# Attention output loaded chunk by chunk a pass ahead, maxima transposed with 128 stationary columns, and VectorE's side work moved within a group

## What is computed

```
x = x + attention(layernorm(x)) @ Wo      # 32 query heads, 8 key/value heads, head size 16,
                                          # rotary embedding, causal mask, softmax over the keys
x = x + (silu(xn @ W_gate.T) * (xn @ W_up.T)) @ W_down.T    # xn = layernorm(x), 1376 hidden features
```

## Time and profile before

| | us |
|---|---|
| median of 3 runs | 799.4 (798.14 to 801.4) |
| the profiled execution | 799.8 |
| its span | 798.1 |
| TensorE busy in it | 763.0 (96%) |
| VectorE busy | 441.1 (55%) |
| ScalarE busy | 341.8 (43%) |
| GpSimd busy | 211.5 (27%) |

### The profile page before, as it was taken

The page is one execution under the profiler, slowest core; times in us unless marked ns, Lnnn a source line. Parts: engine busy times, 40 slices in busy tenths (PEclk is TensorE's granted clock), DMA queues, the critical chain, the costliest instruction groups (busy, mean ns, idle before and its releaser), DMA issues.

```text
span 798.1 us, 12148 instructions
## 1 busy us (share of the span) xinstructions
PE 763.0 (96%) x4240; PEld 507.8 (64%) x4240; DVE 441.1 (55%) x984; ACT 341.8 (43%) x684; POOL 211.5 (27%) x384
## 2 busy tenths in 40 slices
PE   4699999999999997999799999999999999999998
PEld 3545444554444443454588888888878888788886
DVE  7787878788877786996445543233322243231212
ACT  3427767766876776668533222111121111121111
POOL 3326763577446753234300000000000000000000
PEclk9959999999999999899999999999999999999999
DMA  7437777234423436370286101412005120030001
GB/s 263 110 89 247 211 239 217 68 85 121 117 78 100 121 100 197 113 209 27 92 252 181 56 14 52 132 42 65 27 1 168 43 79 26 0 106 0 1 1 53
DMA packets 74613, 81.84 MB, mean 103 GB/s; under 512 B 8720, under 2 KB 58384, under 8 KB 74352
## 3 DMA queue, kind: packets, MB, share of 16 engines
q1 hardware_dynamic: 73264, 79.98, 32.8%
q10 hardware_dynamic: 1296, 1.18, 0.6%
HBM read 57.02 MB, written 33.36 MB: 113 GB/s over the span
## 4 chain that ended last, share of the span: by engine, by line
PE 50%; DVE 0%; issue 0%; DVEq 0%
PE bank L1495 35%; PE ps_y L1547 15%; PE bank L1534 1%; DVE x_in L1477 0%; DVEq L1476 0%
## 5 line engine op out<-in xcount | busy, mean ns | idle before, releaser
L734 ACT ACTIVATE probs<-ps_t 128x512 f32<-128x512 f32 (+1 forms) x352 | 184.2, 562 | 89.9 <-PE ps_t L1145 89.6
L869 DVE CUSTOM_DVE_ANT_0 ps_s<-ps_s,mask_row 128x512 f32<-128x512 f32 (+1 forms) x240 | 145.4, 643 | 42.4 <-PE ps_s L1113 41.2
L1113 PE MATMUL ps_s<-k_rows,q_rows 96*128 96x256 bf16 (+3 forms) x512 | 146.8, 316 | 5.7 <-DMA q_rows<-scratch_q_parts 3.7
L1452 DVE TENSOR_TENSOR h<-h,bank 128x512 f32<-128x512 f32 (+1 forms) x44 | 30.3, 688 | 218.9 <-PE bank L1495 217.7
L1145 PE MATMUL ps_t<-q_rows,k_rows 98*128 98x512 bf16 (+1 forms) x352 | 129.4, 371 | 7.3 <-DMA q_rows<-m_t 4.5
L1390 ACT ACTIVATE h<-bank 128x512 f32<-128x512 f32 (+1 forms) x44 | 26.3, 599 | 149.3 <-PE bank L1495 149.3
L642 POOL TENSOR_SCALAR_AFFINE_SELECT probs<-probs 128x512 f32<-128x512 f32 x128 | 84.4, 659 | 0.0
L873 DVE TENSOR_REDUCE m_raw<-ps_s 128x2 f32<-128x512 f32 (+3 forms) x112 | 73.2, 677 | 19.7 <-PE ps_s L1118 19.2
L1158 PE MATMUL ps_o<-probs,v_ones 128*32 128x512 f32 (+3 forms) x1024 | 82.6, 441 | 0.2 <-ACT o_sb L744 0.2
L1396 ACT CAST h_hi<-h 128x512 fp32r<-128x512 f32 (+1 forms) x44 | 27.3, 621 | 128.4 <-DVE h L1452 128.4
L223 POOL TENSOR_TENSOR var_eps<-mean_var,eps 128x1 f32<-128x1 f32 x16 | 3.1, 191 | 289.6 <-DVE mean_var L218 289.6
(11 more groups left out here) (154 smaller groups left out, 1380.6 us busy)
## 6 DMA issues: line engine op xcount, KB each, us to landing
scratch_o<-o_sb SPq DMA_DIRECT2D x31, 256.0 KB, 2.3
q_rows<-scratch_q_parts SPq DMA_DIRECT2D x32, 192.0 KB
x_in<-in_x SPq DMA_DIRECT2D x16, 256.0 KB, 4.6
q_rows<-scratch_q_parts SPq DMA_DIRECT2D x32, 128.0 KB
x_res<-in_x SPq DMA_DIRECT2D x16, 256.0 KB, 2.7
o_in<-scratch_o SPq DMA_DIRECT2D x64, 64.0 KB
inverse<-scratch_inverse SPq DMA_DIRECT2D x64, 64.0 KB
out<-x_in SPq DMA_DIRECT2D x16, 256.0 KB, 2.1
```

Source lines behind the costliest of these rows:

```text
L734: nc.scalar.activation(probs[:, g % 2, heads * u:heads * (u + 1), CHUNK_AT[c]:CHUNK_AT[c + 1]], ps_t[:, pos % S_BANKS, 0:heads * CHUNK_N[c ...
L869: nc.vector.tensor_tensor_reduce(out=bank, in0=bank, in1=mask_row[:, T - width:T], scale=1.0, scalar=LOWEST, op0=ALU.add, op1=ALU.max, acc ...
L1113: mm = nc.tensor.matmul(bank[:, place], q_rows[r][0:ROWS, j, P * q:P * (q + 1)], k_rows[r][0:ROWS, 0:width], start=(place == 0), stop=mask ...
L1452: nc.vector.tensor_tensor(h[0:m, r], h[0:m, r], bank[units["up", f] % BANKS][0:m, :], ALU.mult).then_inc(h_ready, 1)
```

## The change

The attention output's tiles 0 and 1 of batch 0 are loaded in pass 2, one chunk in a slot, and `wo` and the residual tiles at its slot 20. Tiles 2 and 3 are loaded in the last pass, chunk by chunk from slot 9 and slot 13. The load of the first weights of phase 2 moves from slot 14 to slot 16. `m_parts` gets zeros in 96 more columns, so that the stationary operand of the transposition has 128 and it writes 128 rows, of which 32 are read. The transposition stands behind the dense piece of its place instead of ahead of it. `max_low` comes after VectorE's second maximum of slot 0 instead of after the first. The statistics, mean and application of the layernorm, one third part of rotated rows and the reciprocals move to other slots.

```diff
-LO_SLOT = {7: 0, 13: 1, 15: 2, 22: 3, 25: 4}
+LO_SLOT = {7: 0, 14: 1, 15: 2, 22: 3, 25: 4}
-X_SLOT, STATS_SLOT, MEAN_SLOT, APPLY_SLOT = 26, 8, 12, 18
-SUMS_SLOT, INVERSE_SLOT = 7, 16
-WO_HI, WO_LO, O_LOAD, CTX_SCALE, CTX_HI, CTX_LO = 2, 4, 0, 5, 6, 7
+X_SLOT, MEAN_SLOT = 26, 14
+STATS_AT, APPLY_AT = {6: 0, 7: 1, 10: 2, 11: 3}, {18: 0, 19: 1, 22: 2, 23: 3}
+SUMS_SLOT, INVERSE_SLOT = 7, 18
+WO_HI, WO_LO, CTX_SCALE, CTX_HI, CTX_LO = 2, 4, 5, 6, 7
+WO_LOAD = 20
+O_LOAD_AHEAD = {2: [(0, 0)], 3: [(0, 1)], 6: [(0, 2)], 7: [(0, 3)], 10: [(1, 0)], 11: [(1, 1)], 18: [(1, 2)],
+                19: [(1, 3)]}
+O_LOAD = {9: [(2, 0)], 10: [(2, 1)], 11: [(2, 2), (2, 3)], 13: [(3, 0)], 14: [(3, 1)], 15: [(3, 2), (3, 3)]}
-FFN_LOAD, FFN_HI, FFN_LO = 14, 19, 25
+FFN_LOAD, FFN_HI, FFN_LO = 16, 19, 25
...
+def load_o_chunk(sp, d, to, b, t, c):
     o = d["o"][b].rearrange("g (j s w) t -> s (g j) w t", j=GROUP, s=2)[0]
-    for c in range(KC):
-        heads, at = ...
+    heads, at = slice(P // DH * c, P // DH * (c + 1)), slice(P * t, P * (t + 1))
+    sp.dma_start(to.o_in[:, t % 2, c], o[heads, :, at]).then_inc(to.o_loaded[t % 2], DMA)
+    sp.dma_start(to.inverse[:, t % 2, c], d["inverse"][b, heads, at]....).then_inc(to.o_loaded[t % 2], DMA)
...
-        m_parts = sb("m_parts", [P, 2, 2, GROUP, TT], BF16)
+        m_parts = sb("m_parts", [P, 2, P // (GROUP * TT), GROUP, TT], BF16)
...
+            def prepare_first_tiles(slot):          # SP, in pass B - 2, at the end of each slot
+                if slot == WO_LOAD:
+                    ...                             # wait for raw copies; load wo, residual tiles 0 and 1
+                for t, c in O_LOAD_AHEAD.get(slot, ()):
+                    if (t, c) == (0, 0):
+                        sp.wait_ge(inverse_stored, DMA)
+                    load_o_chunk(sp, d, to, 0, t, c)
...
-                t = (slot - O_LOAD) // TT
-                if slot == O_LOAD + TT * t and t < TT:
-                    if t >= 2:
-                        sp.wait_ge(to.ctx_lo_ready, t - 1)
-                    load_o(sp, d, to, 0, t)
+                for t, c in O_LOAD.get(slot, ()):
+                    sp.wait_ge(to.ctx_lo_ready, t - 1)
+                    load_o_chunk(sp, d, to, 0, t, c)
...
-                    if 0 <= slot - STATS_SLOT < TT:
-                        work.append(lambda: layernorm_stats(b + 2, slot - STATS_SLOT))
+                    if slot in STATS_AT:
+                        work.append(lambda: layernorm_stats(b + 2, STATS_AT[slot]))
...
                     if i == 0 and n + 1 < GROUPS:
-                        others.insert(0, lambda: max_low(n + 1))
+                        others[0:0] = [lambda: None, lambda: max_low(n + 1)]
...
+            nc.vector.memset(m_parts[:, :, 2:], 0.0)
...
-                nc.tensor.matmul(to[0:2 * GROUP * TT, 0:P], m_parts[:, n % 2].rearrange("p w j q -> p (w j q)"),
+                nc.tensor.matmul(to[:, 0:P], m_parts[:, n % 2].rearrange("p w j q -> p (w j q)"),
                                  ident_b[:], start=True, stop=True).then_inc(ready, 1)
...
+                        for place, kind, k, piece in pieces.get((slot, j), ()):
+                            dense(b + 2 if has_next and kind == "T" else b + 1, kind, k, UNIT0[b] + place, piece)
                         if (i, j) == (0, GROUP - 1) and n + 1 < GROUPS:
                             transposed_max(n + 1)
-                        for place, kind, k, piece in pieces.get((slot, j), ()):
-                            dense(b + 2 if has_next and kind == "T" else b + 1, kind, k, UNIT0[b] + place, piece)
```

More of the change, by code:

```diff
@@ L173, in load_o @@
 def load_o(sp, d, to, b, t):
+    for c in range(KC):
+        load_o_chunk(sp, d, to, b, t, c)
+def load_o_chunk(sp, d, to, b, t, c):
     o = d["o"][b].rearrange("g (j s w) t -> s (g j) w t", j=GROUP, s=2)[0]
-    for c in range(KC):
[L177 to L180, removed]
+    heads, at = slice(P // DH * c, P // DH * (c + 1)), slice(P * t, P * (t + 1))
+    sp.dma_start(to.o_in[:, t % 2, c], o[heads, :, at]).then_inc(to.o_loaded[t % 2], DMA)
+    sp.dma_start(to.inverse[:, t % 2, c], d["inverse"][b, heads, at].unsqueeze(1).broadcast_to(
+        [P // DH, DH, P])).then_inc(to.o_loaded[t % 2], DMA)
 def load_residual(sp, d, to, b, t):
@@ L459, in store_inverse @@
                 sp.dma_start(row_inverses(d, b), sums[:]).then_inc(inverse_stored, DMA)
-            def prepare_batch_0(slot):
-                if slot == 0:
+            def prepare_first_tiles(slot):
+                if slot == WO_LOAD:
                     sp.wait_ge(raw_copied, 13 * DMA)
@@ L467, in prepare_batch_0 @@
                     load_residual(sp, d, to, 0, 1)
+                for t, c in O_LOAD_AHEAD.get(slot, ()):
+                    if (t, c) == (0, 0):
+                        sp.wait_ge(inverse_stored, DMA)
+                    load_o_chunk(sp, d, to, 0, t, c)
+            def prepare_batch_0(slot):
                 if slot == FFN_LOAD:
@@ L507, in iteration @@
                         store_inverse(b - 1)
+                    if b == B - 2:
+                        prepare_first_tiles(slot)
                     if not has_next:
@@ L919, in next_work @@
                 if b + 2 < B:
-                    if 0 <= slot - STATS_SLOT < TT:
-                        work.append(lambda: layernorm_stats(b + 2, slot - STATS_SLOT))
+                    if slot in STATS_AT:
+                        work.append(lambda: layernorm_stats(b + 2, STATS_AT[slot]))
                     if slot == MEAN_SLOT:
                         work.append(lambda: layernorm_mean(b + 2))
-                    if 0 <= slot - APPLY_SLOT < TT:
-                        work.append(lambda: layernorm_apply(b + 2, slot - APPLY_SLOT))
+                    if slot in APPLY_AT:
+                        work.append(lambda: layernorm_apply(b + 2, APPLY_AT[slot]))
                     if slot in NEXT_XT:
@@ L1124, in transposed_max @@
                     bank_free(PRE_UNITS - 1, 0)
-                    to, ready = ps_d, dense_ready
+                    to, ready = ps_d[:], dense_ready
                 else:
```

## The result

| | kernel before | changed kernel |
|---|---|---|
| median, us | 799.4 (797.18 to 802.02, 7 runs) | 794.55 (793.08 to 796.36, 7 runs) |
| ratio, 95% interval | | 0.9945 [0.993, 0.996] |
| the profiled execution | 799.8, span 798.1 | 793.49, span 791.8 |
| first matmul of the second phase | at 391.15 | at 384.91 |
| TensorE busy | 763.0 | 753.1 |

The account below looks back on a forecast made before the run. TensorE was taken to bound the kernel, VectorE second. Terms -5.7 - 5.3 + 0.2 + 1.0 = -9.8 us took the profiled 799.8 to 790.0, hence a median of 789.7 us; 8 in 10 between 785.3 and 795.0.

Parts of the forecast that it names:

- term C: Pass 2, attention-output, wo and residual loads ahead of the maxima's transfer in the sixth group: +0.2 us (0 to +1.0).
- Rival 1: In-order queue: small transfers wait for large ones ahead, maxima late in pass 2 (1.0) and last pass (2.0); 791.4 us, 15%.
- rival 4: Stall moves: big transfers hold up the maxima in pass 2 and last pass, 8.2 us per event; 804.8 us, 5%.
- Term D: Last pass, loads of tiles 2 and 3 and first FFN weights: ScalarE and TensorE wait, +1.0 us (0 to 2.0).
- Term A: Maxima's transposition in all passes: 128-column operand and dense piece first save 0.28 us in 22 groups; -5.7 us (0 to -6.6).
- Rival 2: Maxima's transposition: the 0.36 us come from operand type change or the wait, not width; 795.8 us, 8%.
- Term B: First two groups of the last pass: loads a pass ahead remove the 4.09 us stall, VectorE then bounds; -5.3 us.
- Rival 3: Second group of the last pass: VectorE isn't the bound, first out-projection piece at 322.5; 787.2 us, 17%.
- Term E: VectorE's other work in a group's second half changes place, not number: 0 us (-0.3 to +0.5).

Follow-up runs that it names:

- The first two experiments: Changed kernel with wo and residual loads one slot later, behind the maxima's transfer: 789.19 us; the same plus three 2 KB transfers at slot 20: 788.32 us.

## Why the prediction was right or wrong

**The step that failed is term C**, with +4.4 us measured where +0.2 was forecast: "0.9 us late against 2.9 of cover is nothing", and the maxima behind wo landing at 286.9 where the group wants them at 287.0. Put relative to the transposition, the forecast had wo issued 0.1 us after it (279.9 against 279.8), the maxima landed 7.0 after that, and wanted at 7.2: on time by 0.1. Measured were 1.34 (276.27 against 274.93), 9.12 (276.27 to 285.39) and 7.28 (282.21): late by 3.18. Of the error of 3.3, 1.2 is the issue and 2.1 the transfer. The issue came later because SP had no time left: it issues from 262.00 to 278.04 with no gap over 0.4 us, while the groups had shrunk; the maxima of the group before were already issued 3.4 us after their transposition (267.97 against 264.56). The transfer took longer for two reasons: 1024 KB of wo landed 7.6 us after their own issue, and the small transfer came 1.5 us after that (276.27 + 7.6 = 283.9, 285.39). The 7.0 stood for both, and was taken from the FFN weights' two times 768 KB in another stretch; wo itself took 6.1 us in the kernel before and 6.3 to 6.6 behind the maxima's transfer, and why it took 7.6 here is open. The slow clock behind the wait added 1.2 (4.4 less 3.18), which the term had left out altogether. The prediction had the mechanism among its rivals, with the rule of ring order from the Trainium skill, "DMA: Bandwidth & Descriptors", section "Queues, rings and completion order". The first two experiments agree with it. The chance of 15% was the mistake: nothing in the trace spoke for a small transfer that overtakes, and the sum stood on a margin of 0.1 us. Rival 1 had the place right and only 1.0 us for it; rival 4 had the price of an event as 8.2 us, and one such event of 4.4 came.

The sum itself was 0.1 off: its terms give 789.6, not 789.7. And rival 4 weighs -0.2 and 1.3 us where terms C and D have -0.1 and 1.0; neither slip matters.

**Term A was right in mechanism and 1.1 us too small**, 0.2 beyond the -6.6 that was given as its end. The undisturbed regular group gives 0.32 us with both edits and 0.24 with the width alone, against 0.28. The 18 groups 1 to 5, 9 to 13, 17 to 21 and 27 to 29 give 5.06 together, 0.28 each. What was under-sized are the groups 6 to 8, 14 to 16 and 22 to 24, where one pass turns into the next: the sum has some 0.6 us for them (four groups that count in full, less the 0.5 for lateness), and they give 1.75. Of this 0.55 and 0.56 are groups 7 and 15 (from 10.71 and 10.72 to 10.16). Each edit alone gives at most 0.08 there (10.63 and 10.73 with the width, 10.65 twice with the order); why the two together do is open. The Trainium skill, "TensorE: Matmul & The Clock Gate", section "LDWEIGHTS (loading the stationary operand)", gives a load as columns over 1.2 ns, by which an estimate is 27 ns for 32 columns and 107 for 128, so the wide one would cost more; the section on weight-path modes has a fast load for 128 columns that are not FP32. Measured, the wide transposition is the cheaper one by 0.25 us. The measurement decides. Rival 2 said that the width is not what costs: with the width alone 0.25 of the 0.36 us go. Its neighbours have a share too: with the order alone and 32 columns the group is 0.09 to 0.14 us shorter, and with both edits 0.32.

**Term B was right in size, by luck in part.** From the mark of the group before, the first out-projection piece came after 18.35 us (324.11 - 305.76), where the forecast's 324.9 stands for 17.9. The forecast was that VectorE takes TensorE's place as the bound. It does so in the version with wo behind the maxima, where the piece waits for VectorE's low part and comes after 17.26 us, with the clock at 1.00. In the changed kernel's profile VectorE is busy for 4.00 of 4.00 us from 316 to 320, and TensorE waits for its maxima. But then the clock falls to 0.58, which the forecast had ruled out, and the low part is there 1.2 us before the piece:

```profile
322.27 0.68 DVE L213 TENSOR_TENSOR ctx_lo<-o_in,ctx_hi 128x512 fp32r<-128x512 f32 x1
```

VectorE's work was over-sized by 0.6, and the slow TensorE put 1.1 on top. Rival 3 (322.5, here 15.5 us) did not come.

**Term D was right in the profile** (0.9 against 1.0): ScalarE waited 1.61 us for the weights, 1.9 were forecast, and TensorE 0.88 for the maxima. The size is luck in part: the wait at that place was worth 0.9 us in the changed kernel and 4.9 us (a period of 15.25) in the version with wo moved. **Term E** can't be given: from the mark of group 1 to the second phase the two profiles with the old slots take 320.48 and 322.81 us, against 320.79 with the new ones, and the times are 792.41 in one comparison and 788.95 in the other, against 787.85.

## What to carry to other kernels

When a load is moved to fill a hole, look at what stands behind it in its queue, not only at what stands ahead, and ask when each of these is wanted; here a small transfer behind 1.5 MB landed 9.1 us after the first of them was issued. Issue it first and the bulk behind it: here two slots moved by one each, and a stage of ScalarE with them, took a gain of 4.85 us to some 11.6 (ratio 0.9945 to 0.9867), most of it by the first of the two. Do not trust a margin smaller than the spread of the row that it is made of. And measure groups between marks that the change has not moved: the distance of an instruction that the change itself puts elsewhere gives and takes time that nobody won or lost.

## What was not expected of the hardware

- A transposition with 128 stationary columns cost 0.11 us where 32 columns cost 0.36, with the same 128 columns moved.
- 8 KB issued behind 1.5 MB on one queue were there after 7.35 us; behind 6 KB they needed 4.9 at most (277.41 to 282.26).
- The same load at the same place of the same kernel held its successor up by very different amounts from one execution to the next (VectorE waited 2.98 us in one; the group took 11.74 and 14.49 us).
- After waits of 3.2 us the granted clock was 0.60 and 0.63 for some four microseconds. But near 320 us it also was 0.58 after waits of only 0.74, 0.83 and 0.28 us, and after waits of 0.74 and 0.84 at the same place of another version it stayed at 1.00. TensorE had been busy for 2.41 of 4.00 us (316 to 320) in the one and for 2.42 (310 to 314) in the other. The two executions of the kernel with the old slots differ in the same way: 3.04 and 3.05 us busy of 4.00 from 360 to 364, and a clock of 1.00 and of 0.60 from 364 to 368. What made the difference is open.
